# One layer of linear attention and a feed-forward layer on one core: half of the output projection ahead of the products with the state, pieces of the second feed-forward product moved

## The reference

```python
x = x + attn(layernorm(x), ...)      # (4, 2048, 512), 32 heads of 16
x = x + ffn(layernorm(x), W0, bias0, W1, bias1)

# attn: r, k, v, g = mixes of x with its predecessor, times Wr, Wk, Wv, Wg
# chunks of Q = 64 tokens
att = rc @ kc * w_mat
yc = att @ vc + rc @ state * wb
new_state = ws * state + kc * wk @ vc
# y: normalized over each head, * gamma + beta
out = yn * silu(g) @ Wo.T
# ffn: gelu(x16 @ W0.T + bias0) @ W1.T + bias1, hidden 2048
```

## Time and profile before

| | |
|---|---|
| time, median of 3 runs | 2078.05 us (2074.58 to 2080.48) |
| profiled execution | 2075.69 us |
| its span | 2073.9 us |
| PE busy | 2002.3 us, 97% |
| PE weight loads busy | 1423.9 us, 69% |
| DVE busy | 1738.2 us, 84% |
| ACT busy | 1293.5 us, 62% |
| POOL busy | 317.5 us, 15% |
| DMA, main queue | 77.2% of 16 engines' span |

### The profile page before, as it was taken

The page is one execution under the profiler, slowest core; times in us unless marked ns, Lnnn a source line. Parts: engine busy times, 40 slices in busy tenths (PEclk is TensorE's granted clock), DMA queues, the critical chain, the costliest instruction groups (busy, mean ns, idle before and its releaser), DMA issues.

```text
span 2073.9 us, 64752 instructions
## 1 busy us (share of the span) xinstructions
PE 2002.3 (97%) x27206; PEld 1423.9 (69%) x27206; DVE 1738.2 (84%) x3687; ACT 1293.5 (62%) x2081; POOL 317.5 (15%) x329
## 2 busy tenths in 40 slices
PE   5889999999999999999999999999999999999999
PEld 5777667667666767766766776676776667667666
DVE  7778889888888988888988888898888888888761
ACT  7876565676566666655657765666765656666452
POOL 1111111111111111111111111111111111111110
PEclk8999999999999999999999999999999999999999
DMA  6977677888777788777778877778887877887777
GB/s 214 220 199 237 177 236 216 248 239 233 200 233 220 236 241 241 213 226 227 230 231 245 248 203 225 234 215 247 250 231 202 231 220 230 250 238 203 216 249 250
DMA packets 428979, 471.97 MB, mean 228 GB/s; under 512 B 259600, under 2 KB 309392, under 8 KB 428688
## 3 DMA queue, kind: packets, MB, share of 16 engines
q1 hardware_dynamic: 427056, 467.64, 77.2%
q10 hardware_dynamic: 1632, 0.18, 0.1%
HBM read 316.21 MB, written 25.17 MB: 165 GB/s over the span
## 4 chain that ended last, share of the span: by engine, by line
PE 81%; DMA 4%; SPq 4%; DVE 3%; ACT 3%; issue 3%; POOL 0%; ACTq 0%; DVEq 0%
PE F L1132 20%; PE F L1068 17%; PE B L879 10%; PE B L1040 8%; PE sc L879 7%; PE YT L911 6%; PE YT L879 3%; PE YT L963 2%; DMA y<-ygT 2%; PE sc L941 2%; PE YT L982 2%; DMA ring<-w_dram 1%; SPq L2027 1%; PE YT L1012 1%; PE F L836 1%
## 5 line engine op out<-in xcount | busy, mean ns | idle before, releaser
L1132 PE MATMUL F<-ring,hT 128*128 128x512 f16 x1984 | 467.5, 379 | 0.0
L1068 PE MATMUL F<-xT,ring 128*128 128x256 f16 x3840 | 449.3, 273 | 5.1 <-ACT hT L1768 3.7
L1068 PEld LDWEIGHTS F<-xT,ring 128*128 128x128 f16 x3840 | 369.8, 98 | 64.9 <-issue 8.0
L1132 PEld LDWEIGHTS F<-ring,hT 128*128 128x128 f16 x1984 | 189.1, 98 | 197.9 <-issue 0.5
L879 PE MATMUL B<-mix,WT 128*128 128x256 f16 x2304 | 267.5, 273 | 0.4 <-DVE gT L1372 0.3
L1768 ACT ACTIVATE hT<-F,b,f_rho 128x256 f16<-128x256 f32 x480 | 243.5, 560 | 37.9 <-PE F L1068 37.9
L879 PEld LDWEIGHTS B<-mix,WT 128*128 128x128 f16 x2304 | 222.6, 98 | 33.8 <-DVE gT L1372 0.6
L276 DVE SCALAR_TENSOR_TENSOR mixf<-dx,maa,xnT 128x256 f32<-128x256 f32 x512 | 238.6, 526 | 0.1
L1725 ACT ACTIVATE Shl<-S 128x256 f16<-128x256 f32 x128 | 53.1, 415 | 263.7 <-PE YT L982 148.6
L1971 POOL TENSOR_TENSOR Shl<-S,Shl 128x256 f16<-128x256 f32 x128 | 89.2, 697 | 734.7 <-ACT Shl L1725 734.7
L1719 ACT ACTIVATE att<-att 128x512 f16<-128x512 f32 x256 | 147.5, 624 | 68.3 <-DVE att L1333 68.3
(11 more groups left out here) (196 smaller groups left out, 2997.6 us busy)
## 6 DMA issues: line engine op xcount, KB each, us to landing
ring<-w_dram SPq DMA_DIRECT2D x512, 512.0 KB, 4.6
kx<-kT SPq DMA_DIRECT2D x96, 256.0 KB, 3.8
rx<-rT SPq DMA_DIRECT2D x96, 256.0 KB, 4.4
xa<-in_L_attn_x SPq DMA_DIRECT2D x32, 512.0 KB, 7.6
vbd<-vN SPq DMA_DIRECT2D x256, 64.0 KB, 3.1
x<-in_L_attn_x SPq DMA_DIRECT2D x32, 512.0 KB, 6.1
out<-x SPq DMA_DIRECT2D x31, 512.0 KB, 3.8
w_dram<-ring SPq DMA_DIRECT2D x20, 256.0 KB, 3.8
```

The source lines that it names most:

```text
L1068: mm = eng.matmul(up_place(f, j)[:, i * BT:(i + 1) * BT], ring[:, use % RING, i, a * C + kk * P:a * C + (kk + 1) * P], xT[:, :, kk, :], st ...
L1132: mm = eng.matmul(F[:, t, :], hT[:, k, rows(t)], ring[:, use % RING, i, a * C:(a + 1) * C], start=(k == 0 and a == 0), stop=(k == NH - 1 a ...
```

## The change

Only the order of work within a step changes; every instruction stays.

```diff
@@ pe_step
         if ff:
             pe_up(eng, n, 7)
+        if tail:
+            pe_Wo(eng, n, 0)
         if att_n:
             pe_from_state(eng, n, 0)
             pe_scores(eng, n, 2)
             pe_prepare(eng, n, "sc2")
-        if tail:
-            pe_Wo(eng, n, 0)
             pe_prepare(eng, n, "Wo0")
         if ff:
             pe_down(eng, n - 2, 0)
+            pe_down(eng, n - 2, 1)
         if att_n:
             pe_kv(eng, n, 1, n < STEADY)
             pe_scores(eng, n, 3)
@@
-        if ff:
-            pe_down(eng, n - 2, 1)
         if tail:
             pe_Wo(eng, n, 1)
         if ff:
             pe_down(eng, n - 2, 2)
+            pe_down(eng, n - 2, 3)
         if att_n:
             pe_att_v(eng, n, 1)
             pe_from_state(eng, n, 1)
-        if ff:
-            pe_down(eng, n - 2, 3)
@@ dve_steady
         dve_state(eng, n, 1)
+        dve_gate(eng, n, 1)
         if ahead:
             mix_lo(eng, n + 1, 0)
-        dve_gate(eng, n, 1)
+            mix_lo(eng, n + 1, 1)
+        dve_residual(eng, n - 1, 0)
         dve_take_y(eng, n, 0)
         dve_weigh(eng, n, 2)
-        if ahead:
-            mix_lo(eng, n + 1, 1)
         dve_weights_lo(eng, n, 2)
-        dve_variance(eng, n, 0)
-        dve_residual(eng, n - 1, 0)
+        dve_weigh(eng, n, 3)
         dve_state(eng, n, 2)
-        dve_weigh(eng, n, 3)
         dve_weights_lo(eng, n, 3)
         dve_state(eng, n, 3)
+        dve_variance(eng, n, 0)
@@ act_steady
             act_norm(eng, n + 1)
+        act_mix_hi(eng, n, 2)
+        if ahead:
             act_x_words(eng, n + 1)
-        act_mix_hi(eng, n, 2)
@@
+        act_weights_hi(eng, n, 3)
         act_state_hi(eng, n, 2)
-        act_weights_hi(eng, n, 3)
         act_state_hi(eng, n, 3)
```

## The result

The changed kernel takes 2104.9 us (median of four runs, 2098.14 to 2110.20), the kernel before beside it 2076.32; the ratio is 1.0132, 95% interval 1.0110 to 1.0153. The profiled execution took 2102.98 us, its span is 2101.2 us, 27.3 us over that of before. The forecast was slower, 2135 us, in a range of 2092 to 2170: the direction is right and the time is in the range, but the loss is 29 us where the sum had 59 over its base of 2075.7. One term of three was twice too large, and one was missing.

What follows compares the result with a forecast made beforehand. TensorE's own work plus its gaps was taken as the bound. From 2075.7 us, +23 (gelu wait), +59 - 4 (late y transpose) and -19 (instruction loads) gave 2135 us, range 2092 to 2170.

Steps and rivals of the forecast that it cites:

- (a): At the second feed-forward product, TensorE waits 0.8 us for the eighth gelu, behind state_hi, in 30 steps: +23 us.
- (c): Late instruction loads at L941, L982 and L1040 mostly go, from 22.9 to some 4 us: -19 us.
- (b): Piece 3 leaves the step's end; y's transpose comes 2.7 us later, costing 2.1 us a step: +59 us, -4 already counted.
- the prediction's own formula: Delay of y's transpose less 0.60 us before TensorE loses anything, over 28 steps: 2.74 - 0.60 = 2.1 us each.
- A: SyncE's transposes are hidden, its long issues waits for earlier transfers; y adds 0, 2076 us; chance 0.06.
- D: SyncE's queue becomes the bound: late weights for pieces 5 to 7 add 1 to 2 us a step, 2177 us; chance 0.06.
- (d): Remaining swaps, such as residual before take y, cost nothing while VectorE stays ahead; cover a little over 1 us.

Runs made afterwards that it cites:

- e1: The changed kernel with ScalarE's second state_hi moved behind the eighth gelu; ratio 1.0047 to the kernel before, 2088 us.
- e12: The changed kernel with state_hi behind the eighth gelu and piece 3 back at the step's end, run a second time; ratio 1.0003 to the kernel before.
- e2: The changed kernel with piece 3 of the second feed-forward product back at the step's end; ratio 1.0026 to the kernel before, 2085 us.
- e5: The kernel before with piece 7 of the first feed-forward product moved behind from-state and scores of chunk 2; ratio 1.0132, 2114 us.
- e6: The kernel before with kx's three DMAs issued behind x's transpose; ratio 1.0052 to the kernel before.
- e9: The changed kernel with state_hi behind the gelu, piece 3 at the step's end and VectorE's first residual behind the weighing; ratio 1.0092 to the kernel before.
- e11: The changed kernel with y's transpose issued ahead of k's on SyncE's queue; ratio 1.0438 to the kernel before.

## Why the prediction was right in direction and wrong in size

**(a) The eighth gelu behind state_hi: right.** Forecast +23 us in 30 waits of 0.8; measured 21.9 in 28 steps, 30 waits at L1132, with the very times of the earlier trace rows. e1 removes them and none of the other waits, and brings 5.8 us of gaps back.

**(c) The late loads: right in the sum, half right in the reason.** Forecast -19, measured -23.9. That the gaps are instruction loads was right, as the packets show. But I gave the gap to the scores' place and the move of the projection the credit. e12, with the projection moved and PE's two stops repaired, has 14.8 us of gaps behind the next dense stretch; the change, with both stops and with piece 3 ahead of the last products with V, has 1.8. With one of the stops repaired they are 7.6 (e1) and 2.5 us (e2). The Trainium skill ("Runtime: NRT & Kernel Launch", "Instruction fetch mechanics") calls the crossing of a block mostly hidden; 22.9 us here and 44.8 in e5 were not.

**(b) The shift at the step's end: the step that failed.** The chain was right up to the words of x: take y +1.74, row means +1.74, x's transpose +2.5 for 2.74. The step that failed is the sentence that between 420.33 and 433.02 "the queue has no idle that could give 2.7 us back. So y's transpose is 2.7 us later too". I read the 3.87 us of the earlier trace rows as the queue's own work. 1.9 of them were a wait for the transfers ahead, as e6 shows. Of the 2.4 us by which x's transpose is issued later in the mean, its own hold gives back 1.8, and y's transpose came 1.1 us later. The term of +59 - 4 = 55 us measures 25: 19.9 at scores, gate and gelu 4, and 5.0 ahead of piece 7. By the prediction's own formula 1.1 - 0.6 = 0.5 us in 28 steps would be 14 - 4 = 10; that it is 25 means that the centre of the landings against a free ACT was badly chosen as well. The formula treats the wait as if every landing came at one time, while a late landing costs and an early one gives nothing back, and weights behind y are late with it (5.8 us in 8 waits); how the 25 divide between the two is open. Thus two errors of (b) stood against each other: the shift was over twice too large, its price too small, and the term came out only twice too large by that luck. My lower bound (32 - 4 = 28) lay just above the measured 25.

**The first steps** were not in the sum: some +3 us. Moving a step's work in the common list also moved it in steps 1 and 2, whose bound is the preparation of the weights.

With the measured terms: 2075.7 + 22 + 25 - 24 + 3 = 2102, where 2103 was profiled. Of the 33 us between the forecast and this sum, 30 are the term (b). Of the rivals, A ("the queue's long issues may be waits for its own earlier transfers") had the mechanism that I gave 0.06, though only half of its effect. D came in small: 5.8 us of waits for weights. (d) shows no wait in the change; with PE's stops repaired the products with V wait 4.2 us for DVE (e12), and e9 shows what moving the residual costs. No run has the order of DVE alone.

## What to carry to other kernels

Before a shift is passed down a queue, ask what each entry's time on the queue consists of: an issue that takes 3.9 us right behind other DMAs and 2 us elsewhere is partly a wait and absorbs a delay. When work moves past a product, look at every small operation that waits for the product and at what stands behind it on its engine: a 0.4 us copy ahead of a gelu cost 22 us here, and swapping the two won most of it back. And gaps from late instruction loads are set by how densely a whole half step issues, so moving one long product moves the gap; it went away only where PE stopped for something else. Last, a stop can cost more than its length: look at the granted clock and at PE's busy time, not only at the list of waits. The busy time rose by 25 us in e11 with no instruction added.

## What the runs showed of the hardware that I had not expected

A transposing DMA of the same size held SyncE's queue for 1.3 to 3.0 us with nothing of kx just ahead (e6), and for 3.4 to 4.7 us right behind kx's three DMAs (before); in the changed kernel, with kx's three just ahead too but nearer to their landing, for 1.3 to 3.1 us. The starts of the steady steps scatter by up to 5 us with the same first steps (163.4 to 168.9), which is a large part of the 0.3% between executions. And gaps for instructions reached 3.7 us in one piece (e9, L982), longer than the longest 2.5 us of the kernel before. The 14 traces have 46 stretches of TensorE at 1.2 GHz between 200 us and the last 40, and each stands at a single idle of PE of 1.9 to 3.8 us and begins 1.2 to 4.6 us after the idle did. Not every such idle has one: the 2.1 us at L1068 near the end of the changed kernel has none.
